# Turning attention weights compactly, with transfers that build the diagonal operand

## The reference

```
q = x @ Wq;  k, v = split(x @ Wkv)
sim = einsum('bid,bjd->bij', q, k) * scale
sim = sim + cope(q, sim, pos_emb)      # gates, running sum from the end, lookup between two table entries
attn = softmax(sim)
out = einsum('bij,bjd->bid', attn, v)  # per head, per image
h = layernorm(h + out @ Wout + b_out)
h = layernorm(h + routed_experts(h) + shared_expert(h))
```

## Time and profile before

| | us |
|---|---|
| median of three runs | 717.65 |
| the profiled execution | 717.29 |
| its span | 715.5 |
| TensorE busy | 698.0 (98%) |
| TensorE weight loads | 606.4 (85%) |
| VectorE busy | 524.1 (73%) |
| ScalarE busy | 437.4 (61%) |
| GpSimd busy | 122.0 (17%) |

### The profile page before, as it was taken

The page is one execution under the profiler, slowest core; times in us unless marked ns, Lnnn a source line. Parts: engine busy times, 40 slices in busy tenths (PEclk is TensorE's granted clock), DMA queues, the critical chain, the costliest instruction groups (busy, mean ns, idle before and its releaser), DMA issues. The chain is left out here.

```text
span 715.5 us, 14500 instructions
## 1 busy us (share of the span) xinstructions
PE 698.0 (98%) x4930; PEld 606.4 (85%) x4931; DVE 524.1 (73%) x1109; ACT 437.4 (61%) x772; POOL 122.0 (17%) x158
## 2 busy tenths in 40 slices
PE   8999999999999999999999999989998999999995
PEld 5897897979889797988979796868887999998884
DVE  3378998989989898989989898986862222332657
ACT  1565777676776867677686747543216777784453
POOL 2000000000000000000000000010024777775130
PEclk9999999999999999999999999989999999999999
DMA  8620040402304040210402003920004655542811
GB/s 272 225 64 0 2 102 26 102 20 43 76 13 102 25 101 25 61 53 13 94 21 64 25 25 115 345 77 25 3 26 97 146 136 132 147 130 57 287 69 54
DMA packets 75659, 60.79 MB, mean 85 GB/s; under 512 B 49386, under 2 KB 66896, under 8 KB 75628
## 3 DMA queue, kind: packets, MB, share of 16 engines
q1 hardware_dynamic: 71056, 50.35, 26.0%
q0 software_dynamic: 4224, 9.71, 5.1%
q10 hardware_dynamic: 348, 0.34, 0.1%
HBM read 35.40 MB, written 15.54 MB: 71 GB/s over the span
## 5 line engine op out<-in xcount | busy, mean ns | idle before, releaser
L1360 PEld LDWEIGHTS ps_S<-attnT,v_sb 128*128 128x128 f32 x704 | 84.8, 192 | 5.8 <-ACT attnT L1691 3.4
L1360 PE MATMUL ps_S<-attnT,v_sb 128*128 128x128 f32 x704 | 85.8, 275 | 2.5 <-ACT attnT L1691 2.5
L1844 DVE COPY_PREDICATED table<-bit,table 111x112 f32<-111x112 int16 (+6 forms) x110 | 75.0, 682 | 11.2
L775 POOL TENSOR_TENSOR rs<-ve,neg_half 111x2 f32<-111x2 f32 x11 | 12.2, 1113 | 402.4 <-DVE ve L1936 402.4
L971 PE MATMUL ps_X<-wkv_sb,hT 128*111 128x512 f32 (+1 forms) x176 | 80.6, 598 | 0.0
L2280 DVE COPY attnT<-ps_S 128x256 f32<-128x256 f32 x44 | 18.7, 424 | 80.9 <-PE ps_S L1372 80.8
L1015 PE MATMUL ps_X<-oT,wout_sb 128*128 128x222 f32 x320 | 62.0, 350 | 0.0
L1015 PEld LDWEIGHTS ps_X<-oT,wout_sb 128*128 128x128 f32 x320 | 60.0, 190 | 0.0
L878 PE MATMUL ps_S<-hT,wq_sb 128*128 128x216 f32 (+1 forms) x320 | 59.2, 342 | 0.0
L971 PEld LDWEIGHTS ps_X<-wkv_sb,hT 128*111 128x111 f32 (+1 forms) x176 | 28.5, 173 | 35.0 <-issue 34.2
L878 PEld LDWEIGHTS ps_S<-hT,wq_sb 128*128 128x128 f32 x320 | 56.1, 189 | 1.3
(11 more groups left out here) (319 smaller groups left out, 1391.4 us busy)
## 6 DMA issues: line engine op xcount, KB each, us to landing
down_sb<-in_x_dram SPq DMA_DIRECT2D x10, 648.0 KB
gu_sb<-y_d SPq DMA_DIRECT2D x8, 512.0 KB, 6.5
h_d<-hT SPq DMA_DIRECT2D x11, 222.0 KB, 2.6
kept<-h_d SPq DMA_DIRECT2D x11, 222.0 KB, 2.8
h_d<-h SPq DMA_DIRECT2D x10, 222.0 KB
wkv_sb<-in_L_attn_Wkv_dram SPq DMA_DIRECT2D x2, 1024.0 KB, 12.5
gu_sb<-in_L_ffn_gate_w_dram SPq DMA_DIRECT2D x2, 1024.0 KB, 9.7
gu_sb<-in_L_ffn_up_w_dram SPq DMA_DIRECT2D x2, 1024.0 KB, 11.1
```

Source lines behind the costliest of these rows:

```text
L1360: mm = nc.tensor.matmul(S[:, i, j * FF + f * P:j * FF + f * P + P], held[:, i, k, j, f * P:f * P + P], xgT[:, i, k], start=(k == 0), stop= ...
L1844: A.did(V.copy_predicated(near[:, :, :, 0:SL - d], by_side(bit[:, n], r)[:, :, :, 0:SL - d], near[:, :, :, d:SL]))
```

## The change

VectorE writes the weights compactly: one product of `ex` and the inverse sums to `own_attn`, 111 rows by 16 heads by 37; the mask and `rdo` are gone. TensorE turns two heads at a time: a tile of 111 rows by 2 x 37 columns becomes 74 rows by 111. There are eight such transposes into two PSUM banks, and two copies on ScalarE bring them to `turned_attn`, where the first 37 partitions hold the even head and the next 37 the odd head of each pair of heads. Then SyncE issues six transfers (`place_attn`), for each of the two heads and each of the three images: 37 partitions by 8 x 37 numbers, from `turned_attn` to the partitions of that image in `own_T`. This lies in `attnT`, which GpSimd has set to zero once, so that only the diagonal blocks are written. TensorE's `outputs` waits for all six (`placed`). `own_T` has the order image, head, query, so a product reads three runs of 37.

The order changes too. On TensorE the turn of group 2p moves between the first and the second quarter of the next pair's keys, and the outputs of 2p behind the first quarter of the next pair's queries; for odd groups TensorE's order stays. On ScalarE the weights of 2p-1 are copied before the gates, the halves of the image come before the scores of the odd group, the exponential before its gates, and the outputs of 2p and the turned patches move into the next turn. SyncE issues the transfers of 2p-1 after the store of normalised rows and those of 2p after the transpose of the image; at the end the expert weights are loaded after the last pair's transfers. In the last pair shared-expert parts stand before the outputs.

```diff
+        own_attn = attn_flat[:, :HEADS * TOK].rearrange("p (h j) -> p h j", h=HEADS)
+        BLOCKS = HEADS // 2
+        PER_BANK = BLOCKS // 2
+        turned_attn = attn_flat[:, HEADS * TOK:(HEADS + BLOCKS * TPG) * TOK].rearrange("p (b n q) -> p b n q", b=TPG, n=BLOCKS)
+        own_T = attnT[:].rearrange("p h r -> p (h r)").rearrange("p (b h q) -> p b h q", b=TPG, h=HEADS)
...
+        PLACES = 2 * TPG
...
+            def place_attn(p, a):
+                g = p * 2 + a
+                if first(g):
+                    sp.wait_ge(attnT_zeroed, 1)
+                else:
+                    sp.wait_ge(o_done, g * 2)
+                sp.wait_ge(at_sb, g * 4 + 4)
+                apart(sp)
+                for j in range(2):
+                    for b in range(TPG):
+                        sp.dma_start(own_T[TOK * b:TOK * b + TOK, b, j * BLOCKS:j * BLOCKS + BLOCKS],
+                                     turned_attn[TOK * j:TOK * j + TOK, b]).then_inc(placed[a], 16)
...
             with sp.Fori(2, G2 - 4) as p:
                 save_h(p)
                 store_rows(p - 2)
+                place_attn(p - 1, 1)
                 store_halves(p - 2)
                 load_x(p + 3, XR)
                 turn_x(p + 2)
+                place_attn(p, 0)
                 back_h(p)
...
                 for s in range(4):
+                    if s == 1 and not next_first(p):
+                        outputs(p * 2 - 2, 0)
...
                 for s in range(2 if next_first(p) else 0, 4):
+                    if s == 1 and not next_first(p):
+                        turn_weights(p * 2 - 2, True)
...
-                for j, s in enumerate(IN_TURN):
-                    pe.wait_ge(attn_ready, g * 4 + j + 1)
-                    for i in range(4):
-                        mm = nc.tensor.transpose(S[:r, s, i * r:i * r + r], attn[:r, 4 * s + i], ident[:r, :r])
-                    mm.then_inc(at_done, 1)
+                pe.wait_ge(attn_ready, g * 4 + 4)
+                for n in range(BLOCKS):
+                    heads_in = attn_flat[:r, heads_of(n)]
+                    mm = nc.tensor.transpose(S[:heads_in.shape[1], n // PER_BANK, n % PER_BANK * r:n % PER_BANK * r + r],
+                                             heads_in, ident[:r, :r])
+                    if n % PER_BANK == PER_BANK - 1:
+                        mm.then_inc(at_done, 2)
...
             def outputs(g, a):
                 r = rows_of(g)
+                if r == ROWS:
+                    pe.wait_ge(placed[a], (g - a) * (8 * PLACES) + 16 * PLACES)
...
-                            weights = (attnT[:r, odd * FT + f, :r] if r == ROWS
+                            weights = (own_T[:r, :, slot_of(odd * FT + f)] if r == ROWS
...
             def weights(g):
-                for j, s in enumerate(IN_TURN):
-                    act.wait_ge(at_done, g * 4 + j + 1)
-                    nc.scalar.copy(attnT[:ROWS, 4 * s:4 * s + 4, :ROWS],
-                                   S[:ROWS, s, :4 * ROWS].rearrange("p (h r) -> p h r", h=4)
-                                   ).then_inc(at_sb, 1)
+                for j in range(2):
+                    act.wait_ge(at_done, g * 4 + 2 * j + 2)
+                    nc.scalar.copy(turned_attn[:2 * TOK, :, PER_BANK * j:PER_BANK * j + PER_BANK],
+                                   S[:2 * TOK, j, :PER_BANK * ROWS].rearrange("p (n b q) -> p b n q", n=PER_BANK, b=TPG)
+                                   ).then_inc(at_sb, 2)
...
-                N.did(V.tensor_tensor(rdo[:r], rden[:r].unsqueeze(2).to_broadcast([r, HEADS, TPG]),
-                                      own_f[:r].unsqueeze(1).to_broadcast([r, HEADS, TPG]), ALU.mult))
-                N.settle(g)
                 if not first(g):
                     dve.wait_ge(at_done, g * 4)
-                by_head = [r, 4, TPG, TOK]
-                for s in IN_TURN:
-                    of = slice(4 * s, 4 * s + 4)
-                    V.tensor_tensor(attn[:r, of], ex[:r, of].unsqueeze(2).to_broadcast(by_head),
-                                    rdo[:r, of].unsqueeze(3).to_broadcast(by_head), ALU.mult
-                                    ).then_inc(attn_ready, 1)
+                V.tensor_tensor(own_attn[:r], ex[:r], rden[:r].unsqueeze(2).to_broadcast([r, HEADS, TOK]), ALU.mult
+                                ).then_inc(attn_ready, 4)
```

More of the change, by code:

```diff
@@ L330, in vit_tower @@
         o_done = sem("o_done")
+        attnT_zeroed = sem("attnT_zeroed")
+        placed = [sem(f"placed_{a}") for a in range(2)]
         ot_sb = sem("ot_sb")
@@ L613, in _ @@
                 save_h(p)
+                if p == 1:
+                    place_attn(0, 0)
+                    place_attn(0, 1)
                 load_x(p + 3, XR)
@@ L1190, in pair @@
                         turn(c)
-                turn_weights(p * 2, True)
+                if not ahead:
+                    turn_weights(p * 2, True)
                 if ahead:
@@ L1200, in pair @@
                     pe.wait_ge(h1t_sb, FULL)
-                outputs(p * 2, 0)
-                if not ahead:
                     pe.wait_ge(at_sb, 4 * (G - 1))
@@ L1581, in first_pair @@
                 distance(1)
+                patches(2)
                 outputs(0, 0)
-                patches(2)
             def pair(p, ahead, ahead2):
                 if not next_first(p):
-                    for s in range(2):
-                        queries(p, s)
-                if not next_first(p):
-                    for s in range(2, 4):
+                    queries(p, 0)
+                    outputs(p * 2 - 2, 0)
+                    if not last(p):
+                        turned_patches(p + 1)
+                    for s in range(1, 4):
                         queries(p, s)
@@ L1597, in pair @@
                     softmax_exp(p * 2 - 1)
+                else:
+                    weights(p * 2 - 1)
                 gates(p, 0)
@@ L1601, in pair @@
                     split(p - 2)
-                weights(p * 2 - 1)
                 if not ahead:
+                    weights(p * 2 - 1)
                     turn(0)
@@ L1608, in pair @@
                 distance(p * 2)
+                if ahead2:
+                    halves_of_x(p + 2)
                 score(p, 1)
                 tables_out(p, 1)
+                if ahead:
+                    softmax_exp(p * 2)
                 gates(p, 1)
-                if not ahead:
+                if ahead:
+                    keys(p + 1, 0)
+                    weights(p * 2)
+                    for s in range(1, 4):
+                        keys(p + 1, s)
+                    distance(p * 2 + 1)
+                else:
                     for c in range(1, 3):
                         turn(c)
-                softmax_exp(p * 2)
-                if ahead2:
-                    halves_of_x(p + 2)
-                if ahead:
-                    for s in range(4):
-                        keys(p + 1, s)
-                else:
+                    softmax_exp(p * 2)
                     for c in range(3, FULL):
                         turn(c)
-                weights(p * 2)
-                distance(p * 2 + 1)
-                outputs(p * 2, 0)
-                if ahead2:
-                    turned_patches(p + 2)
+                    weights(p * 2)
+                    distance(p * 2 + 1)
+                    outputs(p * 2, 0)
             act.dma_start(pe_nat[:TOK, :], pos_embed[0]).then_inc(w_small, 16)
```

63 lines of the change are left out of this document (35 added, 28 removed).

## The result

The changed kernel takes 969.33 us (median of 4 runs, 966.84 to 971.27) against 718.19 us for the kernel before on the same chip: a ratio of 1.350, with a 95% interval of 1.345 to 1.355. I had forecast 938 us, with a range of 850 to 1030.

What follows compares the result with a forecast made beforehand. TensorE's order of work bounds the kernel, VectorE close behind: 717.3 + 107 (odd groups) + 70 (even) + 10.5 (group 0) + 9 (group 20) + 2 (expert weights) - 17.5 (transposes) + 40 (clock) = 938 us, range 850 to 1030.

Steps and rivals of the forecast that it cites:

- The divisor: Weight transfers: 37 has no divisor up to 16 but one, so all six use one same engine, 11.4 us.
- The chain: From TensorE's turn to complete operand: 0.7 copy + 0.1 wake + 2.0 fixed + 11.4 moving = 14.2 us.
- The stalls: Value products wait for transfers: 10.7 us in odd groups, 7.8 in even, about 10.5 and 9 in groups 0 and 20.
- The transposes: TensorE's turn of the weights: 8 transposes for 16, 0.83 us less for each of 21 groups, 17.5 us.
- The clock: TensorE's granted clock drops after stalls: 2 us lost for each of 20, between 0 and 3.4, 40 us.
- VectorE's slack covers the balance: VectorE waits for gates now behind ScalarE's weight copies; its slack of 3.7 us a turn covers that.
- the expert weights: Their loads come behind the transfers on SyncE, with stores of the halves behind them: 2 us, between 0 and 6.
- The issue: SyncE issues each transfer in 0.24 to 0.31 us, hidden behind the moving.
- spread transfers: Rival: the six transfers spread or overlap, operand complete after 4.9 us; 714 us, down to 705; chance 0.09.
- Six different engines: Rival: each transfer on its own single engine, odd groups wait 2.7 us, even none; 728 us; chance 0.06.

Runs made afterwards that it cites:

- e2_three: Changed kernel with only three of the six transfers issued, the other head of each pair staying zero: ratio 1.1581 to the kernel before.
- e5_pad38: Changed kernel with each head's weights padded from 37 to 38 columns, so transfers have 38 partitions: ratio 1.1562 to the kernel before.
- e5_pad48: Changed kernel with each head's weights padded from 37 to 48 columns, so transfers have 48 partitions: ratio 1.0410 to the kernel before.
- e7_busy_half: Changed kernel with 8 or 11 unread matmuls on TensorE ahead of the value products, just short of the wait: ratio 1.2714 to the kernel before.
- e8_reorder: e5_pad48 with patch embedding ahead of the odd value products and second value projection copied before the turned weights: ratio 1.0203 to the kernel before.
- e10_gates: e8_reorder with the even group's gates ahead of ScalarE's copies and one projection before group 0's products: ratio 1.0027 to the kernel before.
- e11_to_dram: Changed kernel with the six transfers going to DRAM rows, the operand staying zero: 972.46 us in one run, ratio 1.355 to the kernel before.
- e1_split: Changed kernel with each of the six transfers cut in two, of 32 and 5 partitions: ratio 1.1667 to the kernel before.

## Why the prediction was right

- **The divisor.** That each transfer of 37 partitions runs on one engine, and all on the same one, was read from three stores and loads. It held: share 0.07, 25 GB/s, packets one at a time. e2_three shows that the six follow each other on the same engine, and e5_pad38 and e5_pad48 show the cause: with as many transfers and more bytes, another number of partitions alone makes the chain shorter.
- **The chain.** I had 14.2 us from the turn to the operand; it is 14.8. Inside, two errors partly cancel: moving takes 10.7 us, not 11.4, and the part that doesn't depend on the number of transfers is 3.2 us, not 2.0 as taken from the landing of one store. The fit of the Trainium skill that the prediction sets beside it (DMA: Bandwidth & Descriptors, Anatomy of one DMA) is stated there for transfers issued from GpSimd. These are issued from SyncE, and even on sixteen engines (e5_pad48) the chain of the six is 5.2 us, not 2.6.
- **The stalls.** Waits of 10.17 and 7.49 us for 10.7 and 7.8; groups 0 and 20 wait 11.97 and 11.85 where I had 10.5 and 9. The sum is 196.0 us for 196.5. That it is so close is luck: ten odd groups 103.8 for 107 and nine even ones 68.3 for 70 make up for 23.8 in place of 19.5 at the ends, and the odd group's hold-up of 0.80 us, which I had put inside the wait, is booked elsewhere.
- **The transposes.** 0.86 us less a group for 0.83.
- **The clock, mis-sized.** I took 2 us for each of 20 stalls, 40 us, with 3.4 each as the upper bound; it is 61, or 2.9 each for 21. In a turn 5.61 + 6.00 us of TensorE's work run at 0.50, of which half, 5.8 us, is lost. The one case that I had, a tail with an idle stretch of 2.65 us, lost 3.4 us, and I went below it without a reason. e7_busy_half gives back 5.6 us a turn. This is the largest error of the sum, 21 of the 31 us between 938 and 969.
- **What I costed at nothing.** "VectorE's slack covers the balance" held only as long as TensorE stood still: with the chain short, the gate behind the copies was the next limit (e8_reorder to e10_gates, 1.4 us a turn). In the kernel after it costs nothing yet. Two small waits do: the wait of the queries for the last copy of the keys, 0.63 us, I had missed: before, the even products stood between the two. The second value projection's 0.80 us I saw and put inside the wait, where e5_pad48 shows it is real once the chain is short. Together these two are 12.4 of the 12.9 us more of other idle time, which leaves at most 0.5 for the expert weights that I put at 2.
- **The issue.** I took 0.24 to 0.31 us each; from SBUF to SBUF it is 0.54 to 0.62. Behind 10.7 us of moving that costs nothing, and it is 3.7 of 5.2 us once the moving is short.

Of the rivals, spread transfers (714 us) ask for what e5_pad48 had to build by padding. Even then the kernel was 4% slower, which that sum did not see: it left out the small waits and took issues at 0.3 us. (Its lower end is off too: by its own terms, ten turns of 39.6 us give about 701 and not 705.) Six different engines (728 us) are ruled out by the share of 0.07 and by e2_three.

## What to carry to other kernels

Before a DMA goes between two steps of the bound engine, write its chain as issue + fixed + moving and look at what divides its partitions: 37 gave one engine of sixteen, 38 two, and zero rows up to 48 made the step 2.7 times as fast. Then put at least that chain's length of other work beside it, at the ends of the loop too, and restore the order of the engine that feeds the next limit. Here the idle bound engine cost its waits (196 us) and nearly a third again in low clock (61 us), so look at the windows behind a wait, not only at the wait.

## What I had not expected of the hardware

- Issuing a transfer from SBUF to SBUF takes SyncE 0.54 to 0.62 us with 37 to 48 partitions (the first four of six with 37), and 0.66 us on average for alternate ones of 32 and 5; the same shape to DRAM starts at 0.25 (e11_to_dram).
- With six transfers on one engine, the fifth and sixth issue take 1.3 and 2.2 us, and the stores behind them 1.5 to 1.7 us instead of 0.25.
- In waits of 7.5 and 10.2 us TensorE's clock falls to 0.50 before they end, and the low stretches are 10 and 13.7 us long (windows above), with TensorE busy again for 5.6 and 6.0 of them.
- Shorter waits don't all cost clock, and the length of the wait alone doesn't say which do. In e1_split, e2_three and the two padded kernels all waits of 4.5 to 7.6 us are followed by slow products (3.1 to 3.2 us for 1.74), and those of 1.4 us are not; of waits of 2.0 to 3.4 us some are and some are not, even in the same kernel at the same place of the turn. Two turns of e1_split:

```profile
177.17 3.23 PE L1050 MATMUL ps_S<-attnT,v_sb 111*64 111x111 f32 x32 [2.61 <-DMA attnT<-attn]
...
286.43 1.74 PE L1050 MATMUL ps_S<-attnT,v_sb 111*64 111x111 f32 x32 [2.62 <-DMA attnT<-attn]
```
